# Row minima by head in one VectorE instruction, and mamba's head outputs with channels on partitions, in a four-layer kernel on one core

## The reference, cut to what matters

```
y = scan(decay, dt * xh, Bm, Cm) + D_skip * xh      # 8 heads of 64 channels
g = y * silu(z)                                     # 512 channels
u = g * rsqrt(mean(g * g, channels) + 1e-5) * gnorm_w
h = x + u @ out_proj_w
```

## Time and profile before

| | us |
|---|---|
| median of 3 runs | 1370.55 (1367.4 to 1371.41) |
| profiled execution, its own time | 1367.05 |
| its span in the profile | 1365.0 |
| PE busy in the span | 1269.3 |
| VectorE busy | 962.6 |
| ScalarE busy | 788.3 |
| GpSimd busy | 338.6 |

### The profile page before, as it was taken

How to read it: one execution, slowest core, us unless ns; L and a number is a source line. 1 busy time by engine, 2 the same in 40 slices (tenths; PEclk the granted TensorE clock), 3 DMA queues, 4 the chain that set the end, 5 groups by cost and what they waited for, 6 DMA issues and landing times.

```text
span 1365.0 us, 26220 instructions
## 1 busy us (share of the span) xinstructions
PE 1269.3 (93%) x9590; PEld 1006.6 (74%) x9590; DVE 962.6 (71%) x1877; ACT 788.3 (58%) x2690; POOL 338.6 (25%) x766
## 2 busy tenths in 40 slices
PE   6787899999999999999999999999999999988877
PEld 3466778788787778788777778788777777776655
DVE  3655768687787868687787868687787868482633
ACT  3153747475675757475665757475665757564331
POOL 2104131232314131222314131222314131212020
PEclk9899999999999999999999999999999999999898
DMA  8710101001010101001010101001010101000000
GB/s 266 283 43 1 43 1 40 12 8 42 0 46 4 46 4 38 12 8 42 0 46 4 46 4 38 12 8 42 0 46 4 46 4 35 5 5 5 5 4 4
DMA packets 28588, 44.42 MB, mean 33 GB/s; under 512 B 4710, under 2 KB 20614, under 8 KB 28044
## 3 DMA queue, kind: packets, MB, share of 16 engines
q1 hardware_dynamic: 26252, 31.41, 7.2%
q0 software_dynamic: 2304, 12.58, 2.6%
HBM read 37.65 MB, written 6.34 MB: 32 GB/s over the span
## 4 chain that ended last, share of the span: by engine, by line
PE 75%; DVE 14%; ACT 4%; POOL 3%; issue 2%; DMA 1%; SPq 0%; DVEq 0%; another core or an unknown queue 0%; POOLq 0%; ACTq 0%
PE psum L497 47%; PE psum L491 9%; PE psum L657 5%; PE psum L546 2%; PE psum L676 2%; PE psum L709 2%; DVE small_ L1025 2%; PE psum L721 2%; DVE A L1019 2%; DVE A L1033 1%; PE psum L753 1%; PE psum L566 1%; POOL small_ L1301 1%; ACT A L812 1%; DVE A L1110 1%
## 5 line engine op out<-in xcount | busy, mean ns | idle before, releaser
L1301 POOL TENSOR_SCALAR small_<-small_ 128x1 f32<-128x1 f32 x112 | 33.8, 302 | 732.1 <-DVE small_ L1037 354.7
L812 ACT ACTIVATE A<-A,small_ 128x128 f32<-128x128 f32 x384 | 148.6, 399 | 35.2 <-DVE small_ L1026 35.1
L805 ACT ACTIVATE A<-psum 128x1024 f32<-128x1024 f32 (+2 forms) x112 | 76.4, 682 | 119.7 <-PE psum L491 112.3
L491 PE MATMUL psum<-cst,A 128*128 128x128 f32 x672 | 107.0, 284 | 39.9 <-DVE A L1033 20.5
L491 PEld LDWEIGHTS psum<-cst,A 128*128 128x128 f32 x672 | 74.6, 142 | 68.3 <-DVE A L1033 24.7
L812 ACT ACTIVATE ca_p<-ca_p,small_ 128x128 f32<-128x128 f32 x256 | 98.7, 389 | 4.9 <-DVE small_ L1026 4.8
L812 ACT ACTIVATE sa_p<-sa_p,small_ 128x128 f32<-128x128 f32 x256 | 98.7, 388 | 0.8 <-DVE small_ L1026 0.6
L1190 DVE SCALAR_TENSOR_TENSOR A<-psum,half_cw,A 128x127 f32<-128x127 f32 (+2 forms) x288 | 75.2, 340 | 26.2 <-ACT A L916 26.2
L1019 DVE TENSOR_TENSOR A<-psum,cst 128x1024 f32<-128x1024 f32 x32 | 39.2, 1224 | 56.0 <-PE psum L546 54.2
L812 ACT ACTIVATION_READ_ACCUMULATOR A<-A,small_ 128x1 f32 x384 | 76.0, 198 | 0.0
L1302 POOL TENSOR_TENSOR small_<-small_,neg_half 128x1 f32<-128x1 f32 x112 | 67.7, 605 | 9.3
(11 more groups left out here) (219 smaller groups left out, 3214.3 us busy)
## 6 DMA issues: line engine op xcount, KB each, us to landing
inT<-in_tokT SPq DMA_DIRECT2D x16, 256.0 KB, 2.6
kv_rows<-A SPq DMA_DIRECT2D x16, 256.0 KB
ctx_in<-in_ctx SPq DMA_DIRECT2D x16, 128.0 KB, 2.1
A<-bias_rows SPq DMA_DIRECT2D x1, 2048.0 KB, 9.6
Wsakv<-in_wsa_kv SPq DMA_DIRECT2D x1, 2048.0 KB, 11.3
Wcakv<-in_wca_kv SPq DMA_DIRECT2D x1, 2048.0 KB, 9.4
ctx_end<-in_tokT SPq DMA_DIRECT2D x16, 128.0 KB, 2.2
out<-x_out SPq DMA_DIRECT2D x16, 128.0 KB, 1.7
```

The costliest lines, as they stand in the source:

```text
L491: mm = pe.transpose(out[:, c * P:(c + 1) * P], src[:, c * P:(c + 1) * P], ident)
L805: return act.activation(out, in_, ACT.Copy)
L812: ins = act.activation(p[:, h * T:(h + 1) * T], p[:, h * T:(h + 1) * T], ACT.Exp, bias=sm(part, "nm", w * HU + h, w * HU + h + 1), accum_o ...
L1301: then(pool.tensor_scalar(t, src, scale, eps, ALU.mult, ALU.add))
```

## The change

1. Softmax. The scores are made with the opposite sign: queries are scaled by the negative factor, and mask, padding and bias table have their signs turned. `softmax_low` replaces `softmax_max`: per head one `tensor_tensor_reduce` that adds the bias, writes the sum to SBUF and gives the row minimum as an accumulated output. The exponential has scale -1 and the minimum as its bias. The semaphores `negmax` and `added` become one, `lows`, raised after four heads and after eight: ScalarE waits for each half, PE's second product of scores for all eight.
2. Mamba. z is made with channels on partitions. Each head's output is made with channels on partitions too, two heads of 64 above each other. D_skip comes in as a per-partition scalar in `m_gated`, one instruction per 128 channels. The transposes and the copy of `m_back` go. The squares are no longer summed by ScalarE; the new stage `m_sq` sums them on PE against a column of ones, `m_mean` on VectorE scales the sum, GpSimd takes the power. `kv3` on PE waits for `m_ms`, since it writes the PSUM bank of the sum.
3. All four `ORDER` strings are new. `SPARE` is as it was; its entry for `m_back` has no stage any more.

The diff, cut to its core (the sign changes of constants and of the query factors, and the weights' layout, are left out):

```diff
 ORDER = {
-    "PE": "3143412314323143241312412311241344314241412132421414",
-    "Activation": "4343243143144121312314312413214213242414",
-    "DVE": "141221341144432413433423122144421411411431214",
-    "Pool": "4221144141132",
+    "PE": "3143124314323143241312413114214432143421421312421414",
+    "Activation": "434324314314412131312413123142231422414",
+    "DVE": "4123121411444342314334314214442241214141112314",
+    "Pool": "4242113441112",
 }
...
+            def need_lows(t, L, w, half):
+
+                eng.wait_ge(sem[f"{L}_lows"], t.value(2, half + 1) if L == "c3" else t.value(4, 2 * w + half + 1))
...
                     else:
-                        need_unit(t, "l0_added", 0)
+                        need_lows(t, "l0", 0, 1)
...
-                product(Pd, split(xnT3), rows_of(Wmi, 0, DI)).then_inc(sem["m_z"], 1)
+                product_T(Pd, Wmi, 0, DI // P, split(xnT3)).then_inc(sem["m_z"], 1)
...
                 for h in range(HM):
-                    mm = pe.matmul(Pc[:, h * HDM:(h + 1) * HDM], aV[:, h * T:(h + 1) * T], dbx[:, h * HDM:(h + 1) * HDM],
+                    c, e = h // 2, HDM * (h % 2)
+                    mm = pe.matmul(Pc[e:e + HDM, c * T:(c + 1) * T], dbx[:, h * HDM:(h + 1) * HDM], aV[:, h * T:(h + 1) * T],
                                    start=True, stop=True)
                 mm.then_inc(sem["m_y"], 1)
 
-            def m_back(t):
+            def m_sq(t):
+                need(t, "m_gssq")
+                ones = C("upto")[:, T - 1:T]
+                product(Pd[:, 0:1], split(junk3, DI // P), [ones] * (DI // P)).then_inc(sem["m_sq"], 1)
+
+            def m_out(t):
                 need(t, "m_g")
-                turn(Pd, gated, DI // P).then_inc(sem["m_uT"], 1)
-
-            def m_out(t):
-                need(t, "m_uT_sb")
-                product(Pc[:, 0:D], split(uT, DI // P), rows_of(Wmo, 0, D)).then_inc(sem["m_o"], 1)
+                product(Pc[:, 0:D], split(gated, DI // P), rows_of(Wmo, 0, D)).then_inc(sem["m_o"], 1)
...
+                need(t, "m_ms")
...
-                need_unit(t, f"{L}_negmax", w)
                 for h in range(HU):
-                    ins = act.activation(p[:, h * T:(h + 1) * T], p[:, h * T:(h + 1) * T], ACT.Exp,
+                    if h % (HU // 2) == 0:
+                        need_lows(t, L, w, h // (HU // 2))
+                    ins = act.activation(p[:, h * T:(h + 1) * T], p[:, h * T:(h + 1) * T], ACT.Exp, scale=-1.0,
...
-                act.activation(junk3, gated, ACT.Square, accum_out=sm(4, "ssq1")).then_inc(sem["m_gssq"], 1)
-
-            def m_uT(t):
-                need(t, "m_uT")
-                copy(uT, Pd).then_inc(sem["m_uT_sb"], 1)
+                act.activation(junk3, gated, ACT.Square).then_inc(sem["m_gssq"], 1)
...
-            def softmax_max(t, L, w, p, scores, extra):
-
-                mx, nm = (sm(PART[L], name, w * HU, (w + 1) * HU) for name in ("mx", "nm"))
+            def softmax_low(t, L, w, p, scores, extra):
+
                 need_unit(t, f"{L}_scores", w)
-                ins = dve.tensor_tensor(heads(p), heads(scores), extra, ALU.add)
-                if L == "c3":
-                    then(ins)
-                else:
-                    ins.then_inc(sem[f"{L}_added"], 1)
-                    need_unit(t, f"{L}_added", w)
-                then(dve.tensor_reduce(mx, heads(p), AX.X, ALU.max))
-                dve.tensor_scalar(nm, mx, -1.0, None, ALU.mult).then_inc(sem[f"{L}_negmax"], 1)
+                held()
+                for h in range(HU):
+                    at = slice(h * T, (h + 1) * T)
+                    ins = dve.tensor_tensor_reduce(p[:, at], scores[:, at], extra(h), 1.0, TOP, ALU.add, ALU.min,
+                                                   sm(PART[L], "nm", w * HU + h, w * HU + h + 1))
+                    if h % (HU // 2) == HU // 2 - 1:
+                        ins.then_inc(sem[f"{L}_lows"], 1)
...
-                dve.tensor_tensor(heads(xD, HM), xh, each(pr("D_skip"), HDM), ALU.mult)
...
-                then(dve.tensor_tensor(gated, xD, Pc, ALU.add))
+                for c in range(DI // P):
+                    at = slice(c * T, (c + 1) * T)
+                    ins = dve.scalar_tensor_tensor(gated[:, at], xbcT[:, at], pc("D_skip", c), Pc[:, at], ALU.mult, ALU.add)
+                then(ins)
                 dve.scalar_tensor_tensor(gated, gated, 0.5, sz, ALU.mult, ALU.mult).then_inc(sem["m_g"], 1)
+
+            def m_mean(t):
+                need(t, "m_sq")
+                dve.tensor_scalar(sm(4, "ssq1"), Pd[:, 0:1], 1.0 / DI, 1e-5, ALU.mult, ALU.add).then_inc(sem["m_ms"], 1)
...
-                need(t, "m_gssq")
-                rsqrt(4, sm(4, "r1"), sm(4, "ssq1"), 1.0 / DI, 1e-5, "m_grstd")
+                need(t, "m_ms")
+                pool.tensor_tensor(sm(4, "r1"), sm(4, "ssq1"), neg_half[:, 0:1], ALU.pow).then_inc(sem["m_grstd"], 1)
```

More of the change, by code:

```diff
@@ L25 @@
 NEG = -1.0e9
+TOP = 3.0e38
 LOG_A_CAP = 80.0
@@ L106 @@
 PART4 = ["m_squares", "m_hat", "m_dtz", "m_xbc", "m_tap0", "m_tap1", "m_tap2", "m_tap3", "m_silu", "m_seg", "m_xh", "m_heads",
-         "m_back", "m_out", "kv3", "hat3", "q3", "c3_s", "c3_p", "c3_m", "c3_out"]
+         "m_sq", "m_out", "kv3", "hat3", "q3", "c3_s", "c3_p", "c3_m", "c3_out"]
 PARTS = {1: PART1, 2: PART2, 3: PART3, 4: PART4}
@@ L170 @@
 ]
-NAMES += [f"{L}_{step}" for L in ("l0", "sa", "ca", "c3") for step in ("scores", "negmax", "exp", "probs", "PT", "PTsb")]
-NAMES += ["l0_added", "sa_added", "ca_added"]
+NAMES += [f"{L}_{step}" for L in ("l0", "sa", "ca", "c3") for step in ("scores", "lows", "exp", "probs", "PT", "PTsb")]
 def build(nc, tokT, ctx, idx, pad, cols, rows, consts, setup, rel, w0_q, w0_k, w0_v, w0_o, w0_g, w1_q, w1_kv, w1_o,
@@ L485, in _ @@
             pe.sem_inc(sem["c3_kv"], 1)
-            need, free, need_unit = need_by(pe)
+            need, free, need_unit, need_lows = need_by(pe)
             def turn(out, src, n):
@@ L782, in _ @@
                 "m_hat": [m_turn], "m_dtz": [m_dtz], "m_xbc": [m_xbc], "m_seg": [m_seg], "m_xh": [m_xh],
-                "m_heads": [m_heads], "m_back": [m_back], "m_out": [m_out], "kv3": [kv3], "hat3": [turn3], "q3": [query3],
+                "m_heads": [m_heads], "m_sq": [m_sq], "m_out": [m_out], "kv3": [kv3], "hat3": [turn3], "q3": [query3],
                 "c3_s": [scores3], "c3_p": [turn_probs3], "c3_m": [mix3], "c3_out": [project3],
@@ L953, in _ @@
                 "m_squares": [m_squares], "m_hat": [m_norm], "m_dtz": [m_gate], "m_tap0": [m_last_tap], "m_tap3": [m_tanh],
-                "m_seg": [m_decay], "m_heads": [m_gsquares], "m_back": [m_uT], "hat3": [norm3],
+                "m_seg": [m_decay], "m_heads": [m_gsquares], "hat3": [norm3],
                 "c3_s": [lambda t: softmax(t, "c3", 0, probs3)], "c3_p": [turned3], "c3_m": [mixed3],
@@ L962, in _ @@
             steps = [0]
-            need, free, need_unit = need_by(dve)
+            need, free, need_unit, need_lows = need_by(dve)
             def step(ins):
@@ L1248, in _ @@
                 "inputs": [inputs], "kv0": [project0],
-                **{f"l0_s{w}": [lambda t, w=w: softmax_max(t, "l0", w, probs0[w], P_1, spread(C("window"), HU))] for w in range(2)},
+                **{f"l0_s{w}": [lambda t, w=w: softmax_low(t, "l0", w, probs0[w], P_1, lambda h: C("window"))] for w in range(2)},
                 **{f"l0_p{w}": [lambda t, w=w: softmax_norm(t, "l0", w, probs0[w])] for w in range(2)},
@@ L1255, in _ @@
                 "m_silu": [m_silu],
-                "m_xh": [m_mix], "m_heads": [m_gated], "m_out": [result_m], "kv3": [keys_values3], "hat3": [normed3],
-                "q3": [query3], "c3_s": [lambda t: softmax_max(t, "c3", 0, probs3, P_4, spread(pad_add[:], HU))],
+                "m_xh": [m_mix], "m_heads": [m_gated], "m_sq": [m_mean], "m_out": [result_m], "kv3": [keys_values3], "hat3": [normed3],
+                "q3": [query3], "c3_s": [lambda t: softmax_low(t, "c3", 0, probs3, P_4, lambda h: pad_add[:])],
                 "c3_p": [lambda t: softmax_norm(t, "c3", 0, probs3)], "c3_out": [result3],
@@ L1414, in _ @@
                 "fold1": [fold1], "fold4": [fold4],
-                "m_squares": [m_rms], "m_xbc": [m_steps], "m_heads": [m_grms], "m_out": [deviation3],
+                "m_squares": [m_rms], "m_xbc": [m_steps], "m_sq": [m_grms], "m_out": [deviation3],
             }
```

46 lines of the change are left out of this document (25 added, 21 removed).

## The result

The kernel after takes 1319.93 us in the median of four runs (1317.21 to 1322.45), against 1368.97 us for the kernel before in the same comparison: ratio 0.9646 (95% interval 0.961 to 0.9682). The forecast was 1345 us, range 1326 to 1370. The sign was right and the gain twice as large as forecast: 49 us, not 24.

What follows compares the result with a forecast made beforehand. PE's queue was taken to set the 76.56 us round, with VectorE late at two places. Rounds of 75.4 give -15 in thirteen, outside the loop -7.3: from 1367.05 to 1344.8, said as 1345 us, range 1326 to 1370.

Steps and rivals of the forecast that it cites:

- The price of a head: VectorE's time per head's row minimum in the softmax: 0.33 us taken, between 0.20 and 0.51; 2.7 us for eight.
- the wait of 0.9 before `sa_p0`: In each loop round PE would wait 0.9 us for VectorE before `sa_p0`'s transposes; 0.3 at 0.26 a head.
- Rival C: VectorE keeps up at 0.26 a head: rounds of 74.8 us, 1335 in total; chance 0.26. At 0.20 with cheap `m_sq`: 1326.
- PE's sum: PE's work in a loop round: 74.98 us less 0.88 (`m_heads`), less 0.50 (`m_back`), plus 0.88 (`m_sq`), making 74.5.
- The wait before `c3_p`: PE's 1.20 us wait for VectorE's normalization before `c3_p`'s eight transposes in each round would go in the new order.
- the stretch 7.4 against 6.2: From the end of `c3_s`, PE reaches `c3_p` after 7.4 us; VectorE's normalized product is ready at 6.2.
- Halves: ScalarE may begin exponentials after four minima, 1.4 us instead of 2.67, so a row is ready 1.3 us sooner.
- Outside the loop: Closing -2.6 us, draining -2.5, the phase before it -1.2, opening and filling -1: -7.3 together.
- The clock: After the loop PE's clock may stay lower without `m_back`'s two spare matmuls: 2 us allowed in the range.
- A, serialized accumulators: Accumulated outputs serialize VectorE at 0.51 a head: rounds of 79.6 us, total 1404, slower; chance 0.11.
- B, other waits in full: Other waits replace the removed ones, leaving only PE's savings: -0.5 in each of 13 rounds and -7, 1355 at most; chance 0.14.
- D, no change at 0.38 to 0.42: VectorE's minimum costs 0.38 to 0.42 us a head, leaving the total at 1363 to 1372 us; chance 0.09.

Runs made afterwards that it cites:

- the two fillers: Kernel after with two small unread VectorE additions behind each head's minimum, heads 0.42 us apart: 1379.47 us, ratio 1.0091 against the kernel before.
- the fillers: Kernel after with one or two small unread VectorE additions behind each head's minimum: 1342.3 us with one, 1379.47 with two.

## Why the prediction was wrong

**The price of a head is the step that failed most.** The text took 0.33 between bounds of 0.20 and 0.51, "nearest" to the 0.26 of a fused instruction from PSUM plus 0.07 for the accumulator. It is 0.21. The lower bound's working (0.29 for the work, less the overlap) was the right one; the 0.26 row was of another form, and the 0.07 was added for an instruction that starts together with the next head's. At 0.21 the wait of 0.9 before `sa_p0` is gone, as the forecast's own rule gives; that is 11.7 of the 17.6 us that the forecast lacks in the loop. With this term alone put right the forecast is 1333, inside its range; two smaller ones, PE's work (5.9 us) and the stretches outside the loop (4.8), carry the time below 1326. Rival C had the price at 0.20, with a round of 74.1 and 1326 us, and its low end was set as the range's bound. That its round fits the measured 74.05 is partly luck: it rests on an `m_sq` at half its price, and `m_sq` cost the full 0.88; the starts of the next paragraph made up for it.

**PE's sum was 74.5 and is 74.05.** The terms for `m_heads` (-0.88 taken, -0.80 measured), `m_back` (-0.50) and `m_sq` (+0.88) hold. The rest, 0.45 a round or 5.9 us, lay mainly in what was called work: starts that were late by 0.1 to 0.25 without a row in the list of waits, as that of `center0` behind `q3`.

**The wait before `c3_p` went,** and the stretch 7.4 against 6.2 was read rightly. But the reason that the removed waits do not come back is the new softmax, its quicker minima and its halves: with the new order and the old softmax PE waits 1.4 us for the copy to `sa_k` instead (order only, 77.39). The forecast priced the order and the minima together and did not say that one needs the other.

**Halves.** The text said of the first exponential that it comes 1.3 us sooner and used it in the tail and for `c3_p`. It had `sa_m` wait for the copy behind the exponentials only at a price of 0.40, and did not ask what the halves save there. At a price of 0.32 it is worth 1.91 us a round in the loop; at 0.21 its worth was not measured.

**Outside the loop** -7.3 was forecast, -12.1 measured (11.5 of it after the loop). By stages, with mamba's first product in each phase as the mark: the phase of three parts 72.3 to 70.5 (-1.8; forecast -1.2), draining 60.0 to 53.8 (-6.2; forecast -2.5), closing 53.9 to 50.3 (-3.6; forecast -2.6). The mis-sized term is draining: it was given the closing batch's steps, and the minima alone shorten it by 5.4 (to 54.6). It also has `ca_s0` and `ca_s1`, whose exponentials start sooner too; that these make the difference is my reading and was not tested. In closing, `m_sq` and its wait eat what `m_heads` and `m_back` return: from `m_heads` to `kv3` it was 8.84 before and is 8.99. The clock, named as a risk of 2 us, fell in the kernel after and cost 2.6; it had been at half in `m_out` before as well. The closing batch of before also ran `m_dtz`'s first product at half the clock, 3.9 us to the next start where the kernel after needs 2.3; that is another part of the -3.6 which no step of the forecast had.

**The rivals.** A, serialized accumulators: refuted, 0.21 and not 0.51; its consequence, slower from about 0.40 on, was shown by the two fillers (0.42). B, other waits in full: refuted in the kernel after, where PE has no listed wait; with the order alone other waits do replace the removed ones, and more than in full (2.9 us a round against 1.6). D, no change at 0.38 to 0.42: the fillers put that price between the two kernels measured, 1342 at 0.32 and 1379 at 0.42.

## What to carry to other kernels

Price a VectorE instruction by the distance of starts of independent neighbours, not by its duration, with an accumulated output inside that distance and not on top of the duration; where two bounds of a repeated price lie far apart, give the forecast's range the whole result at each. A new order of queues is worth what the durations under it allow: it lost 0.83 us a round with the old softmax and won 1.07 with the new one and the new mamba part (0.53 with the old), so test it with the change, never alone. In a tail, put spare products where a stage was added and PE now waits, and before a product is moved, ask what it covered.

## What the runs showed of the hardware

- A VectorE instruction of 128x128 fp32 from PSUM with an accumulated output leaves two records (0.286 and 0.083 us) and costs 0.211 from start to start; a small addition behind it adds 0.10 (714.85 to 714.95), two add 0.21 (heads 0.42 apart).
- An fp32 matmul with 128 weight columns costs 0.22 us with one moving column and 0.23 with 64.
- A PE idle time of 2.61 us was followed by 5.28 us at a granted clock of 0.50; 2.4 us of spare products in it kept the clock at 1.00. An idle time of 1.67 or 1.68 us before the same work was followed by a fall (granted 0.62 over 4.50 us) in four of 13 rounds and by none in nine.
- The same instructions ahead of the loop took 178.0 to 183.0 us in four profiles, the longest with the lowest granted clock there (0.90). Single profiles of a few us difference say nothing of that stretch.
